# Second layer: scores for the row maxima from high halves only, two query tiles on the two halves of the array's rows

## The reference

```python
xn = rms_norm(x, gamma)
qkv = xn @ w_qkv            # 16 heads of 64
sim = (q * 64 ** -0.5) @ k.T
attn = softmax(sim)
out = (attn @ v) @ w_out
```

## Time and profile before

| | before |
|---|---|
| median of three runs | 2931.93 us |
| the profiled execution | 2933.54 us |
| its span | 2931.8 us |
| TensorE, matmuls | 2763.0 us busy (94%), 13570 |
| DVE | 2102.1 us (72%) |
| ACT | 1857.1 us (63%) |
| POOL | 1969.5 us (67%) |
| mean granted clock of TensorE | 0.979 |
| second layer | from about 692 us to the end |

### The profile page before, as it was taken

How to read it: one execution, slowest core, us unless ns; L and a number is a source line. 1 busy time by engine, 2 the same in 40 slices (tenths; PEclk the granted TensorE clock), 3 DMA queues, 4 the chain that set the end, 5 groups by cost and what they waited for, 6 DMA issues and landing times.

```text
span 2931.8 us, 46455 instructions
## 1 busy us (share of the span) xinstructions
PE 2763.0 (94%) x13570; PEld 2044.7 (70%) x13570; DVE 2102.1 (72%) x3548; ACT 1857.1 (63%) x2682; POOL 1969.5 (67%) x1177
## 2 busy tenths in 40 slices
PE   6889798785999999999999999999999999999997
PEld 4555498674677777777777777777777777777775
DVE  6878776786677777777777777777777777777774
ACT  4555332234677777777777777777777777777774
POOL 4667610771676777777777777777777777777775
PEclk8999999898999999999999999999999999999998
DMA  4442388894222222322221222222222222132221
GB/s 132 142 144 97 133 264 266 273 309 152 51 51 56 65 63 48 72 44 65 50 68 43 72 52 59 54 65 63 47 73 44 65 50 68 43 72 52 60 56 43
DMA packets 251933, 266.18 MB, mean 91 GB/s; under 512 B 96064, under 2 KB 196672, under 8 KB 251712
## 3 DMA queue, kind: packets, MB, share of 16 engines
q1 hardware_dynamic: 239552, 231.47, 29.8%
q0 software_dynamic: 12288, 33.57, 3.6%
HBM read 123.37 MB, written 73.92 MB: 67 GB/s over the span
## 4 chain that ended last, share of the span: by engine, by line
PE 72%; ACT 1%; DVE 1%; POOL 1%; DMA 1%; issue 0%; SPq 0%; POOLq 0%; ACTq 0%; DVEq 0%
PE psV_b L1653 8%; PE psV_b L1648 8%; PE psV_b L1649 8%; PE psS_b L1636 8%; PE psS_b L1635 8%; PE psN_b L1621 8%; PE psY_b L1576 4%; PE psX_b L1576 4%; PE psY_b L1578 4%; PE psY_b L1577 4%; PE psX_b L1577 4%; PE psX_b L1578 4%; POOL pp_lo_b L1340 1%; PE psN_b L1705 1%; DVE vals_lo_b L1539 0%
## 5 line engine op out<-in xcount | busy, mean ns | idle before, releaser
L1340 POOL TENSOR_TENSOR pp_lo_b<-pf_b,pp_hi_b 128x1024 fp32r<-128x1024 f32 x512 | 1237.3, 2417 | 596.0 <-ACT pp_hi_b L1386 509.5
L1498 DVE TENSOR_REDUCE negmax_b<-psN_b 128x2 fp32r<-128x1024 f32 x512 | 626.9, 1224 | 332.1 <-PE psN_b L1621 324.4
L1381 ACT ACTIVATE pf_b<-psS_b 128x1024 f32<-128x1024 f32 x512 | 526.1, 1028 | 225.2 <-PE psS_b L1636 222.1
L1635 PE MATMUL psS_b<-qA_b,kA_b 128*128 128x512 f32 x1024 | 405.8, 396 | 7.7 <-DVE qB_b L1522 4.5
L1636 PE MATMUL psS_b<-qB_b,kB_b 68*128 68x512 f32 x1024 | 406.7, 397 | 0.0
L1649 PE MATMUL psV_b<-pp_hi_b,vals_lo_b 128*64 128x512 f32 x1024 | 403.8, 394 | 0.0
L1648 PE MATMUL psV_b<-pp_hi_b,vals_hi_b 128*65 128x512 f32 x1024 | 402.0, 393 | 1.5
L1405 ACT ACTIVATE kA_b<-psX_b 64x512 fp32r<-64x512 f32 x256 | 152.0, 594 | 289.7 <-PE psX_b L1578 284.8
L1621 PE MATMUL psN_b<-kA_b,qA_b 128*128 128x512 f32 x1024 | 322.8, 396 | 5.1 <-DVE negmax_b L1498 4.7
L1653 PE MATMUL psV_b<-pp_lo_b,vals_hi_b 128*65 128x512 f32 x1024 | 320.3, 394 | 5.0 <-POOL pp_lo_b L1340 5.0
L1386 ACT ACTIVATE pp_hi_b<-pf_b 128x1024 fp32r<-128x1024 f32 x256 | 271.6, 1061 | 8.1
(11 more groups left out here) (215 smaller groups left out, 5620.7 us busy)
## 6 DMA issues: line engine op xcount, KB each, us to landing
kA_b<-kA_b SPq DMA_DIRECT2D x128, 256.0 KB, 3.1
qB_b<-qA_b SPq DMA_DIRECT2D x128, 256.0 KB, 2.9
inverse_b<-inverse_dram SPq DMA_DIRECT2D x256, 128.0 KB, 2.9
xs_e<-rows_dram SPq DMA_DIRECT2D x144, 128.0 KB, 3.5
results_dram<-ys_e SPq DMA_DIRECT2D x72, 256.0 KB, 3.8
x_a<-x_dram SPq DMA_DIRECT2D x16, 512.0 KB, 4.8
part_dram<-x_s SPq DMA_DIRECT2D x32, 256.0 KB, 2.1
acc_s<-part_dram SPq DMA_DIRECT2D x32, 256.0 KB, 5.1
```

Source lines behind the costliest of these rows:

```text
L1340: pool.tensor_tensor(pp[1][:, c], pf[:, c], pp[0][:, c].bitcast(F32), ALU.subtract).then_inc(pl_pool, 1)
L1381: a.activation(pf[:, c], psS[:], ACT.Exp).then_inc(exp_act, 1)
L1498: v.tensor_reduce(negmax[:, n.slot(2), 2 * c:2 * c + 2], psN[:], AX.X, ALU.max, negate=True).then_inc(mx_dve, 1)
L1635: pe.matmul(psS[:, t], kA[:, s, keys], qA[:, s], start=True, stop=False)
```

## The change

The scores for the maxima are made of the high halves alone (64 rows in place of 128), and the two query tiles of a call are given to the two halves of the array's rows: tile 0 reads `qA` and `kA` on partitions 0 to 63, tile 1 reads `qB` and `kA` on 64 to 127. For this q's copy in `qB` moves to partitions 64 to 127, k low in `kB` too, the four rows of maxima and ones move to partitions 0 to 3, and partitions 4 to 63 are zero. What is subtracted in the softmax is now the maximum of the high-by-high scores. L1636 has 128 rows. The call c = 0 waits for the head's own copy of q (`dup_q[j]`) where it waited for DVE's low part of q; `scores_t` the other way round. The copy of q is issued in two halves with a counter each. ACT makes the two qA parts ahead of the two reads of `psV`. Two tiles are set to zero at the start of the layer. In the first layer three counters of the end are merged into others.

```diff
-        kB = sb("kB", [DH + TB, 4, S], F32R)
-
-        qB = sb("qB", [DH + TB, 4, S], F32R)
+        kB = sb("kB", [P, 4, S], F32R)
+
+        qB = sb("qB", [P, 4, S], F32R)
+        top, low_half = slice(0, DH), slice(DH, 2 * DH)
...
@@ -1281,8 +1281,10 @@
                 if g.const % 2 == 0:
                     spread_sums(g)
                 if p is not None:
-                    after(sp, kq_act, 4, p, 4)
-                    sp.dma_start(qB[0:DH, two].bitcast(F32), qA[0:DH, two].bitcast(F32)).then_inc(dup_q, 16)
+                    for j in range(2):
+                        slot = 2 * p.slot(2) + j
+                        after(sp, kq_act, 4, p, 3 + j)
+                        sp.dma_start(qB[low_half, slot].bitcast(F32), qA[top, slot].bitcast(F32)).then_inc(dup_q[j], 16)
...
+            pool.memset(qB[top].bitcast(F32), 0.0).then_inc(ready, 1)
...
@@ -1414,6 +1417,10 @@
                     exp(0)
                     high()
                     exp(1)
+                if p is not None:
+                    after(a, kq_pe, 2, p, 2)
+                    part(qA, 0, DH ** -0.5)
+                    part(qA, 1, DH ** -0.5)
                 m = g + -1
                 if m.within(0, NH):
 
@@ -1424,10 +1431,6 @@
                     after(a, nm_pool, 1, q + -2, 1)
                     a.activation(inverse[other, r], psV[total, m.slot(2)], ACT.Copy).then_inc(nm_act, 1)
                     a.activation(outs[mine, r], psV[values, m.slot(2)], ACT.Copy).then_inc(nm_act, 1)
-                if p is not None:
-                    after(a, kq_pe, 2, p, 2)
-                    part(qA, 0, DH ** -0.5)
-                    part(qA, 1, DH ** -0.5)
...
@@ -1457,10 +1460,12 @@
         @block.vector
         def _(v):
-            v.memset(kB[DH:DH + TB].bitcast(F32), 1.0).then_inc(const_dve, 1)
             v.wait_ge(gamma_in, 16 * KD)
-            v.tensor_scalar(gamma1[:], gamma1[:], 1.0, None, ALU.add).then_inc(const_dve, 1)
-            v.wait_ge(const_dve, 2)
+            v.tensor_scalar(gamma1[:], gamma1[:], 1.0, None, ALU.add).then_inc(gamma_dve, 1)
+            v.memset(kB[top].bitcast(F32), 0.0).then_inc(const_dve, 1)
+            v.wait_ge(const_dve, 1)
+            v.memset(kB[0:TB].bitcast(F32), 1.0).then_inc(const_dve, 1)
+            v.wait_ge(gamma_dve, 1)
...
@@ -1612,13 +1617,13 @@
                 if c == 0:
                     p = pair_at(n, 0)
                     after(pe, dup_k, 16, p, 16)
-                    after(pe, kq_dve, 4, p, 4)
+                    after(pe, dup_q[n.const % 2], 16, p, 16)
                     after(pe, mr_dve, 1, n + -1, 1)
                 else:
                     after(pe, mx_dve, 2, n, 1)
                 for t in range(2):
-                    i = 2 * c + t
-                    mm = pe.matmul(psN[:, t], qA[:, s, i * P:(i + 1) * P], kA[:, s], start=True, stop=True)
+                    i, (rows, left) = 2 * c + t, ((top, qA), (low_half, qB))[t]
+                    mm = pe.matmul(psN[:, t], left[rows, s, i * P:(i + 1) * P], kA[rows, s], start=True, stop=True)
                 mm.then_inc(sn_pe, 1)
 
             def scores_t(g, c):
@@ -1626,7 +1631,7 @@
                 s = g.slot(4)
                 if c == 0:
                     after(pe, mr_dve, 1, g, 1)
-                    after(pe, dup_q, 16, pair_at(g, 0), 16)
+                    after(pe, kq_dve, 4, pair_at(g, 0), 4)
                     after(pe, exp_act, 2, g + -1, 2)
```

## The result

The changed kernel takes **3125.47 us** (median of 4 runs, 3123.57 to 3130.59), the kernel before beside it 2930.60 (2928.79 to 2936.22): ratio 1.0659, 95% interval 1.0643 to 1.0675. The forecast was 3136 us within 3030 to 3225. The profiled execution took 3123.57 us with a span of 3121.8, 190.0 more than before.

A forecast was written before the change was run, and what follows sets the result against it. TensorE, busy 199.8 of 200 us in the second layer, was taken as the bound. Adding 69 us for calls, 132 for the stall and 2 for the layer's start to 2933.5 gave 3136 us, range 3030 to 3225.

The forecast's parts named there:

- two prices: On TensorE, switching between 64-row and 128-row matmuls, 69 us, and standing for the copy of q, 132 us.
- The calls of a step: Both L1621 calls on TensorE: standstills and bare weight loads outweigh the saved stream, 0.27 us a step, 69 us added.
- The stall: Call 0 of a pair's first head waits 1.05 us for q's copy, held behind spread on SP: 126 times, 132 us.
- L1621 waits for nothing: Sign in the profile that the forecast stall, L1621 waiting some 126 times about 1 us for q's copy, is wrong.
- Who else waits: Other users of ACT's new order, psV's reads, POOL and DVE's maximum: nothing added.
- 128 rows in L1641 for 68: L1636 before the edit, going from 68 to 128 rows at the same 512 columns: same pitch, nothing added.
- Start of the layer: Second layer's start: one more memset on DVE and the first call 0 waiting for its copy, together 2 us.
- E: Rival: an fp32r pair on the array does not run at once, 108 us more, 3233 us; chance 0.03.
- F: Rival: TensorE's granted clock falls to a mean of 0.95, 110 us more, 3235 us; chance 0.03.
- B: Rival: q's copy lands before TensorE is ready for it, so no stall, 3004 us; chance 0.05.
- C: Rival: no switch cost for fp32r on TensorE, but the stall is there, 2973 us; chance 0.05.
- D: Rival: neither switch cost nor stall; 64-row pairs load under the stream ahead, copy in time, 2816 us; chance 0.04.

The follow-up runs named there:

- the kernel without the stall: Changed kernel with the two halves of q's copy issued ahead of the transfer for spread on SP: 2988.61 us, ratio 1.0196 to the kernel before.
- 64-row run: Kernel before with the scores for the maxima contracted over the 64 high rows alone, both tiles on the same array half, one after the other: 3123.29 us, ratio 1.0637.
- 68-row runs: Kernel before with the scores for the maxima contracted over rows 0 to 67 of qA and kA: 2935.50 us, ratio 0.9991.
- the run with 128-row scores: Changed kernel with both score tiles again 128 rows of qA and kA, the copy wait kept, a wait for q's low part added: 3101.20 us, ratio 1.0579.
- the run with the pair twice: Changed kernel with q's copy ahead of spread on SP and each call's 64-row pair issued twice into the same banks: 3143.78 us, ratio 1.0713.

## Why the prediction was right, point by point

The forecast's sign, its two prices and its sum held: 194.9 us measured between the medians, 203 forecast. That the sum came so near is in part luck: the two prices came out lower than forecast, by 12 and by some 8 us, and a term of 16 us was missing. The terms, one by one:

1. **The calls of a step: 69 us forecast, 57 measured** (the kernel without the stall, 1.0196, which also holds the start of the layer). That fp32r pays as fp32 does is shown by the bare loads in the timeline and by the 64-row and 68-row runs. The size taken for one call was met. From the last matmul of `scores_t` to the stream behind the call, the medians over the whole trace are 0.70 us in the kernel before (0.69 was taken), and without the stall 0.81 with the weighing behind and 0.86 with kq or shared work behind: (0.11 + 0.16) x 256 = 69 us. Summed from start to start over all calls the two traces differ by 60 us, and 6 us of that come back in term 4; where the 9 us between the two ways of counting lie is open.
2. **The stall: 1.05 us in 126 pairs, 132 us forecast; 126 waits of 0.92 us booked, 116 us.** Counted as the forecast counts, from where the load could have started, it is 0.95 us in the timeline above; from the last matmul of `scores_t` to the call the traces with and without the stall differ by 124 us in sum. The chain was the one forecast: ACT's qA at kq's end, L1432 behind it, SP's issue of spread, the copy 0.61 us later, the landing. Dated from kq's end, spread left 1.75 us later (forecast 1.91, since L1432 starts before the second part's record ends), the copy 2.36 (2.55), and the landing took 2.3 us (2.2). Removing the stall on SP alone or on ACT alone gave the same 2988 us. One sign of being wrong, "L1621 waits for nothing", is what the profile books literally ("issue"); the landing 0.02 us ahead of the load and these two runs show that it is the copy.
3. **Who else waits: "nothing" was wrong.** It was the step that failed. The forecast gave the maximum "its usual time" and asked only whether the next call would have to wait for it; what is queued behind the maximum on DVE it didn't ask. The low part of the next batch's rows is, and TensorE waits for it 15 times: 16 us, shown by moving that one instruction.
4. **128 rows in L1641 for 68: not quite nothing, but in favour.** The starts of neighbours within `scores_t` are 0.234 us apart on average where L1636 has 68 rows (the kernel before, the run with 68 rows) and 0.231 where L1641 has 128 (the changed kernel, the run with 128-row scores): some 6 us less in all. Why isn't shown.
5. **Start of the layer: 2 us.** It wasn't run by itself and is within the runs' spread.

Three sums of the forecast don't come out, and none touches its range: by its own terms the shorter stream gives 62 us and not 58, E 3136 + 108 = 3244 us and not 3233, F 3136 + 110 = 3246 and not 3235.

The rivals: without the stall (B) 3004 was forecast for what 2988 is, which is the kernel with the copy moved. C and D fell with the bare loads and the 64-row run, E with starts 0.01 us apart, F with the granted clock of 1.00 from 1000 to 1200 us (0.983 over the whole run, 0.979 before). The rule of the Trainium skill (TensorEngine Tiling, section Key Properties) that a change of mode drains the engine is borne out here for fp32r, with 0.09 us on each side. The Trainium skill (TensorE: Matmul & The Clock Gate, Part 3) lists a weight load as overlapping with matmuls in flight only where the row group differs. The trace doesn't agree:

```profile
1809.12 0.19 PEld L1626 LDWEIGHTS psN_b<-kA_b,qA_b 64*128 64x128 f32 x1
```

That is the second pair's load in the run with the pair twice. It starts with the first pair's streams at 1809.12, on the same rows; likewise the load of L1641 at 1803.25 starts with the matmul ahead on all 128 rows. Loads are bare at the ends of a stretch of the mode, and not inside it.

## What to carry to other kernels

Half-array matmuls are bought with an entry and an exit: here 0.09 us of standstill and a bare weight load each, 0.35 to 0.40 us in all, more than the one 512-column stream of 0.23 us that a pair saves. Collect at least two pairs between an entry and an exit; that was tried only with each pair made twice, and gave 19 us. Where the halves are not to run at once, a few rows more are free: 68 rows paid nothing. When a new consumer is put on a transfer, read the issuing queue in program order: an instruction that was moved on one engine can hold another's queue, and neither order is to blame alone. And when a wait is added, list what is queued behind everything that it delays, on each engine down the chain.

Neither kernel is beaten here. One stretch of four tiles in each step would cost, by the intervals above, 0.20 + 2 x 0.23 + 0.15 = 0.81 us for 0.94 now, some 30 us of the whole as an estimate; it needs four banks for the scores where the kernel has two, and wasn't tried.

## What the runs showed of the hardware

- An instruction of DVE that subtracts one tile in SBUF from another and an instruction of POOL that does the same don't run side by side. Begun 0.35 us behind POOL's, DVE's took 2.59 us for 0.68 (2.58 to 2.62 in each of the 15 batches); begun 0.08 us ahead, it made POOL's 2.87 us of 2.38. All 30 of DVE's subtractions into xT_lo, in the trace before and in the one after, began under an instruction of POOL and ended 0.55 to 0.58 us behind its end, whatever was left of it at the start. That was read from traces; no run took the overlap away by itself. The Trainium skill (SBUF — State Buffer, section SBUF: two separate sides) calls the port pair that DVE and GpSimd share a lock that the first comer holds for its whole instruction; the timelines agree in both directions. An instruction that is a little late can so become much later.
- 64 rows cost more than 68: 3123 against 2935 us for the same instructions otherwise.
- The name that the profile gives a wait can be missing: the stall is booked as "issue" in the changed kernel (126 waits, 116.2 us), and to the DMA by name in the run with 128-row scores (116 waits, 136.4 us, and 11 as "issue"). Why isn't shown. Date such a wait by the landing.
